# Last two expert tiles kept in SBUF and summed by TensorE, and adjacency loop numbers packed into one register load

## The reference

```python
edge_index = jnp.stack([src, dst])
xn = _layernorm(x, axis=-1)
x = x + _L0_gnn_ref(xn, edge_index, ...) + _L0_mix_ref(xn[None], ...)[0]
x = x + _L0_ffn_ref(_layernorm(x, axis=-1)[None], ...)[0]
...
x = x + _L3_ffn_ref(_layernorm(x, axis=-1)[None], ...)[0]
```

```python
top_w, top_idx = jax.lax.top_k(gate_weights, TOP_K)      # TOP_K = 2 of 8
combine = combine.at[jnp.arange(T)[:, None], top_idx].add(softmax(top_w))
for e in range(E):
    out = out + combine[:, e:e + 1] * (gelu(xf @ we1[e] + be1[e]) @ we2[e] + be2[e])
```

## Time and profile before

| | us |
|---|---|
| median of 3 runs | 3020.09 |
| profiled execution | 3023.55 |
| its span | 3021.8 |
| PE matmuls busy | 2625.2 |
| DVE busy | 1713.8 |
| ACT busy | 1170.1 |
| POOL busy | 1214.3 |
| adjacency, first to last one-hot | 12.7 to 158.5 |
| end of routed layer 1 (last tile scaled) | 2156.1 |
| end of routed layer 2 | 2632.5 |
| end of routed layer 3 | 2982.1 |

### The profile page before, as it was taken

How to read it: one execution, slowest core, us unless ns; L and a number is a source line. 1 busy time by engine, 2 the same in 40 slices (tenths; PEclk the granted TensorE clock), 3 DMA queues, 4 the chain that set the end, 5 groups by cost and what they waited for, 6 DMA issues and landing times. The chain is left out here.

```text
span 3021.8 us, 46495 instructions
## 1 busy us (share of the span) xinstructions
PE 2625.2 (87%) x16977; PEld 1700.5 (56%) x16977; DVE 1713.8 (57%) x3387; ACT 1170.1 (39%) x2632; POOL 1214.3 (40%) x1469
## 2 busy tenths in 40 slices
PE   8899889999978989989898977999699959769684
PEld 5555558556556855545554645777346646445462
DVE  7776778724687863766535353222336376554743
ACT  6454457423546633322412242444232325432141
POOL 0121677877277788855304212111004226510042
PEclk9999999999999999989998987999799979979897
DMA  2001345443044544424101008999701049720297
GB/s 52 14 22 61 112 147 153 137 122 101 32 136 145 156 129 123 126 91 126 39 8 42 28 16 329 412 414 416 247 1 43 29 148 323 252 63 1 70 379 253
DMA packets 164807, 415.38 MB, mean 137 GB/s; under 512 B 24027, under 2 KB 75771, under 8 KB 141356
## 3 DMA queue, kind: packets, MB, share of 16 engines
q1 hardware_dynamic: 150077, 362.10, 35.6%
q0 software_dynamic: 12960, 42.48, 3.7%
q10 hardware_dynamic: 1555, 7.95, 1.1%
HBM read 325.37 MB, written 87.09 MB: 136 GB/s over the span
## 5 line engine op out<-in xcount | busy, mean ns | idle before, releaser
L2924 POOL TENSOR_SCALAR raw<-raw 128x512 f32<-128x512 f32 x376 | 267.2, 711 | 928.6 <-PE ps L527 297.2
L545 PE MATMUL ps<-units,ARENA 128*125 128x512 f16 x2760 | 617.6, 385 | 16.2 <-POOL units L2928 11.4
L527 PE MATMUL ps<-ARENA,units 128*128 128x500 f16 (+1 forms) x2952 | 540.0, 345 | 22.7 <-ACT tmp L1511 6.0
L545 PEld LDWEIGHTS ps<-units,ARENA 128*125 128x125 f16 x2760 | 375.1, 139 | 243.9 <-DVE X L2578 16.4
L527 PEld LDWEIGHTS ps<-ARENA,units 128*128 128x128 f16 x2952 | 289.7, 99 | 271.1 <-issue 22.0
L1969 DVE TENSOR_TENSOR ARENA<-tmp,ARENA 128x500 f16<-128x500 f32 (+3 forms) x237 | 172.1, 732 | 379.2 <-ACT ARENA L1437 191.8
L2928 POOL TENSOR_TENSOR AT<-raw,AT 128x512 f16<-128x512 f32 x200 | 242.2, 1211 | 17.0
L2928 POOL TENSOR_TENSOR units<-raw,units 128x512 f16<-128x512 f32 x188 | 230.4, 1226 | 16.0
L1436 ACT ACTIVATE tmp<-ps,cols 128x500 f32<-128x500 f32 (+1 forms) x144 | 87.5, 608 | 352.2 <-PE ps L527 343.6
L2977 POOL DMA_INDIRECT picks_d<-ARENA,proj x81 | 82.0, 1013 | 341.3 <-DVE ARENA L2421 341.3
L1033 PE MATMUL ps<-ARENA 128*128 128x128 f16 x3240 | 192.0, 220 | 2.2 <-DVE ARENA L2412 2.0
(11 more groups left out here) (480 smaller groups left out, 4479.7 us busy)
## 6 DMA issues: line engine op xcount, KB each, us to landing
ARENA<-split_d SPq DMA_DIRECT2D x135, 1024.0 KB
raw<-in_moe SPq DMA_DIRECT2D x200, 256.0 KB, 3.0
split_d<-AT SPq DMA_DIRECT2D x200, 256.0 KB, 2.5
raw<-in_units SPq DMA_DIRECT2D x188, 256.0 KB, 2.5
ARENA<-split_d SPq DMA_DIRECT2D x27, 1280.0 KB
rows_d<-ARENA SPq DMA_DIRECT2D x6, 896.0 KB
ARENA<-picks_d SPq DMA_DIRECT2D x6, 896.0 KB
ARENA<-picks_d ACTq DMA_DIRECT2D x6, 896.0 KB
```

The costliest lines, as they stand in the source:

```text
L527: ins = pe.matmul(o[:, 0:nt * R], wt, mv_, start=(i == 0), stop=(i == len(steps) - 1))
L545: ins = pe.matmul(o[0:R, :], th(srcT, h, k, t, 1), w(k, g), start=(i == 0), stop=(i == len(steps) - 1))
L2924: pool.tensor_scalar(r, r, WEIGHT_SCALE, gain, ALU.mult, ALU.mult).then_inc(sem("pool_step"), 1)
```

## The change

The packed numbers: one f32 sum per `dt` (first + 128 x groups + 8192 x before) is made by the three matmuls into one row, cast once, and each engine loads one register per `dt` and takes the three numbers out of it with a mask and two shifts. POOL splits unit 0 only after `tables` is 2. The last two tiles (25, 26) are not scattered. ACT writes their weighted high part in f16, DVE the low part (with the sign of high minus low turned by the order of operands: the sum of both is the value), and DVE makes two maps (125 columns for each token tile, 1 where the slot's token is that column's) once at tile 20. The reload of the picks waits for tiles 23 and 24, goes into other buffers (AT for token tiles 0 to 4, ARENA for 5 to 9, the latter after the ring slots there are free), and comes in chunks of 3, 2 and 5. The first 3 token tiles (5 in layer 3) are still added to X by DVE as they arrive. PE then makes for each token tile the sum of both kept tiles through the maps (4 f16 matmuls of 512 columns), and for the rest of the token tiles also both reloaded picks through the f32 identity (2 f32 matmuls of 512 columns); DVE adds PE's bank to X, one instruction per token tile.

```diff
-PICK_CHUNKS = [(0, 2), (2, 4), (6, 4)]
+PICK_CHUNKS = [(0, 3), (3, 2), (5, 5)]
+KEPT = [TILES - 2, TILES - 1]
+FIRST_HALF = T // 2
+MAPS_AT = 20
+SUMMED_BY_DVE = {1: 3, 2: 3, 3: 5}
+SECOND_HALF_AT = {1: 6144, 2: 5120, 3: 0}
...
+        def span_values(eng, dt):
+            packed = eng.value_load(span_i[:, dt:dt + 1], min_val=128, max_val=(T * GROUPS + 1) * 8192)
+            return (packed & 127).with_bounds(...), ((packed >> 7) & 63).with_bounds(...), (packed >> 13).with_bounds(...)
...
         def load_picks(eng, layer, k):
-            for g in (TILES - 2, TILES - 1):
+            for g in (KEPT[0] - 2, KEPT[0] - 1):
                 eng.wait_ge(sem(f"picks_stored{g % 2}"), 16 * pick_stores(layer, g))
             for c, (t0, nt) in enumerate(PICK_CHUNKS):
+                if t0 == FIRST_HALF:
+                    ...
+                        eng.wait_ge(sem(last[0]), last[1])        # ring slots under the second half
...
-            for i, (v, table) in enumerate(((span_first, ident[0:T, 0:T]), (span_len, ident[0:T, 0:T]), (span_len, tri_tiles))):
-                ins = pe.matmul(o[0:1, i * T:(i + 1) * T], v, table, start=True, stop=True)
+            for i, (v, table) in enumerate(((span_first, ident[0:T, 0:T]), (span_len128, ident[0:T, 0:T]), (span_len, tri_tiles))):
+                ins = pe.matmul(o[0:1, 0:T], v, table, start=(i == 0), stop=(i == 2))
...
+            def token_sums(layer, tiles):
+                if 0 in tiles:
+                    pe.wait_ge(sem("routing_step"), s.more("routing_step", 1))
+                    pe.wait_ge(sem("tile_y"), layer * TILES)
+                for t in tiles:
+                    by_dve = t < SUMMED_BY_DVE[layer]
+                    if not by_dve:
+                        chunk = [c for c, (t0, _) in enumerate(PICK_CHUNKS) if t0 <= t][-1]
+                        pe.wait_ge(sem(f"picks_back{chunk}"), 16 * 2 * len(PARTITION_CUTS) * layer)
+                    pe.wait_ge(*left("dve"))
+                    o = bank("dve", "result" if layer == 3 else "read_dve")
+                    for i in range(2):
+                        for h in range(2):
+                            ins = pe.matmul(o[0:R, :], token_maps[layer][i][:, t * R:(t + 1) * R], kept_y[i][:, h, :], ...)
+                    if not by_dve:
+                        for k in range(2):
+                            ins = pe.matmul(o[0:R, :], ident[0:R, 0:R], back(layer, k, t), start=False, stop=(k == 1))
+                    ins.then_inc(sem("filled_dve"), 1)
...
             routed_hidden(1)
+            token_sums(1, range(0, 7))
...
                     for part in range(2):
                         for c, (t0, nt) in enumerate(CH):
                             pe.matmul(columns[k][c][:, 0:nt * R], xs(part, q)[...], at(q, t0 * R, (t0 + nt) * R), ...)
+                    if k == 0 and q < 3:
+                        token_sums(1, [7 + q])
...
             routed_normed()
+            token_sums(2, range(0, 7))
             for k in range(KC):
                 transposed_group(M, "normed", 0, k)
+            token_sums(2, range(7, T))
...
             routed_hidden(3)
+            token_sums(3, range(T))
...
+            def kept_hi(layer, i):
+                act.wait_ge(sem("filled_dve"), kept_banks[layer, KEPT[i]])
+                act.wait_ge(sem(f"picks_stored{KEPT[i] % 2}"), 16 * pick_stores(layer, KEPT[i] - 2))
+                act.activation(kept_y[i][:, 0, :], o[:, :], ACT.Identity, scale=kept_w[:, i:i + 1]).then_inc(sem("tile_hi"), ...)
...
             routed_hidden(1, ACT.Gelu)
+            kept_hi(1, 0)
             load_picks(act, 1, 1)
+            kept_hi(1, 1)
...
-            then(dve.tensor_copy(spans, o[0:1, 0:3 * T]))
-            dve.tensor_copy(span_i[0], spans[:, 0:T])
-            dve.tensor_copy(span_i[1], spans[:, T:2 * T])
-            dve.tensor_copy(span_i[2], spans[:, 2 * T:3 * T]).then_inc(sem("spans"), s.one("spans"))
+            dve.tensor_copy(span_i, o[0:1, 0:T]).then_inc(sem("spans"), s.one("spans"))
...
             def tile_out(layer, g):
...
+                if g in KEPT:
+                    i = g - KEPT[0]
+                    dve.wait_ge(sem("tile_hi"), s.more("tile_hi"))
+                    stt(kept_y[i][:, 1, :], o[:, :], kept_w[:, i:i + 1], kept_y[i][:, 0, :], ALU.mult, ALU.subtract).then_inc(sem("tile_y"), ...)
+                    return
...
+            def early_picks(layer, tiles):
+                for t in tiles:
+                    dve.wait_ge(sem(f"picks_back{chunk}"), 16 * 2 * len(PARTITION_CUTS) * layer)
+                    for k in range(2):
+                        tt(nat(X, t), nat(X, t), back(layer, k, t), ALU.add).then_inc(sem("dve_step"), ...)
+                        dve.wait_ge(*s.latest())
...
                     if g >= 1:
                         tile_out(layer, g - 1)
+                    if g == MAPS_AT:
+                        token_columns(layer)
+                    if g == TILES - 1 and layer == 1:
+                        early_picks(layer, range(SUMMED_BY_DVE[layer]))
+                if layer == 3:
+                    early_picks(layer, range(SUMMED_BY_DVE[layer]))
...
-                        tt(nat(X, t), nat(X, t), nat(back[0], t), ALU.add).then_inc(sem("dve_step"), s.one("dve_step"))
-                        dve.wait_ge(*s.latest())
-                        tt(nat(X, t), nat(X, t), nat(back[1], t), ALU.add).then_inc(sem(name), s.one(name))
+                    dve.wait_ge(sem("filled_dve"), s.more("filled_dve"))
+                    tt(nat(X, t), nat(X, t), s.bank("dve")[0:R, :], ALU.add).then_inc(sem(name), s.one(name))
...
                     if g >= lag:
-                        scatter(g - lag)
+                        if g - lag not in KEPT:
+                            scatter(g - lag)
...
+                if u == 0:
+                    pool.wait_ge(sem("tables"), 2)
```

More of the change, by code:

```diff
@@ L352, in build, with back @@
         mean_sq = ARENA[:, 14408:14409]
-        back = [YT[:, :], ARENA[:, 2 * T * D:3 * T * D]]
+        kept_w = proj[:, 0, 436:438]
+        kept_y = [tile_y[g % 2].bitcast(F16).rearrange("p (h n) -> p h n", h=2) for g in KEPT]
+        token_iota = K[:, 2048:2048 + N // 2].bitcast(F16)
+        token_maps = {layer: [(tmp.rearrange("p i n -> p (i n)") if layer == 2 else K[:, 2673:2673 + N])[:, i * N // 2:(i + 1) * N // 2].bitcast(F16) for i in range(2)]
+                      for layer in (1, 2, 3)}
+        def back(layer, k, t, n=1, p0=0, p1=R):
+            if t < FIRST_HALF:
+                a = XSEL_END + (k * FIRST_HALF + t) * D
+                return AT[p0:p1, a:a + n * D]
+            a = SECOND_HALF_AT[layer] + (k * FIRST_HALF + t - FIRST_HALF) * D
+            return ARENA[p0:p1, a:a + n * D]
+        kept_banks = {}
         unit_release = []
@@ L362, in pick_stores @@
         def pick_stores(layer, g):
-            return (layer - 1) * (TILES - TILES // 2 if g % 2 == 0 else TILES // 2) + g // 2 + 1
+            return (layer - 1) * sum(i % 2 == g % 2 for i in range(TILES - len(KEPT))) + g // 2 + 1
         marks = {}
@@ L398, in load_picks @@
         def load_picks(eng, layer, k):
-            for g in (TILES - 2, TILES - 1):
+            for g in (KEPT[0] - 2, KEPT[0] - 1):
                 eng.wait_ge(sem(f"picks_stored{g % 2}"), 16 * pick_stores(layer, g))
             for c, (t0, nt) in enumerate(PICK_CHUNKS):
+                if t0 == FIRST_HALF:
+                    width = L2_COLS if layer == 2 else 2048
+                    for slot in range(SECOND_HALF_AT[layer] // width, (SECOND_HALF_AT[layer] + 2 * FIRST_HALF * D - 1) // width + 1):
+                        last = [use[4] for use in ring_uses if use[0] == layer and use[1] == slot][-1]
+                        eng.wait_ge(sem(last[0]), last[1])
                 for p0, p1 in PARTITION_CUTS:
-                    eng.dma_start(back[k][p0:p1, t0 * D:(t0 + nt) * D].rearrange("p (t d) -> p t d", t=nt),
+                    eng.dma_start(back(layer, k, t0, nt, p0, p1).rearrange("p (t d) -> p t d", t=nt),
                                   picks_d[k * PICK:k * PICK + N, :].rearrange("(p t) d -> p t d", t=T)[p0:p1, t0:t0 + nt, :])\
@@ L1695, in tile_hi @@
                 act.activation(tile_T[g % 2][:, 0, :, :].rearrange("p k n -> p (k n)"), o[:, :], ACT.Identity).then_inc(sem("tile_hi"), s.one("tile_hi"))
+            def kept_hi(layer, i):
+                act.wait_ge(sem("filled_dve"), kept_banks[layer, KEPT[i]])
+                o = PS[RING["dve"][(kept_banks[layer, KEPT[i]] - 1) % len(RING["dve"])]]
+                act.wait_ge(sem(f"picks_stored{KEPT[i] % 2}"), 16 * pick_stores(layer, KEPT[i] - 2))
+                act.activation(kept_y[i][:, 0, :], o[:, :], ACT.Identity, scale=kept_w[:, i:i + 1]).then_inc(sem("tile_hi"), s.one("tile_hi"))
             def routed_hidden(layer, func):
@@ L1751, in routed_normed @@
                         gelu_squares(h2_rows[(g - 1) % 2], ss2[(g - 1) % 2])
+                    if g == TILES:
```

(4 more changed lines are left out.)

56 lines of the change are left out of this document (33 added, 23 removed).

## The result

| | before | after |
|---|---|---|
| median of 20 runs each, us | 3018.23 | 3006.18 |
| lowest and highest | 3010.80, 3030.53 | 3000.04, 3017.07 |
| ratio, 95% interval | | 0.9965 (0.9953 to 0.9976) |
| span of the profiled execution | 3021.8 | 3004.4 |
| mean granted clock | 0.936 | 0.946 |

What follows compares the result with a forecast made beforehand. PE's matmuls fill 87% of the span, so time is gained only where PE stands still or is paced by others. -6.3 - 5.9 + 6.8 - 4 - 1 = -10.4 from 3020.09: 3009.7 us, range 3000 to 3026.

Steps and rivals of the forecast that it cites:

- POOL out of the adjacency: Adjacency: the tile beside POOL's split of unit 0 falls from 18.67 to 12.33 us; -6.3 us (bounds -7 and -3).
- one load for three: Adjacency: fewer register loads save 0.55 us in each of 9 tiles and 0.9 at the start; -5.9 us.
- layer 1: End of routed layer 1: earlier reload and PE's sums end the block near 2201.5 instead of 2205.3; -4 us.
- layer 2: End of routed layer 2: last chunk about 2653 instead of 2661, third projected tile about as before; -1 us.
- layer 3: End of layer 3: reload issued 4.3 us earlier, but five PE sums follow the last chunk; net +6.8 us.
- Rival (a): Adjacency: masks and shifts eat the loads' gain, at 0.84 us of register work per tile; 3015.6 us, chance 0.17.
- DVE's own saving adds nothing: Adjacency, change of tile: PE's path is the longer one, so DVE's fewer loads give no time.
- by the reload's price the first chunk is there at about 2160: Layer 1: first chunk, three tiles from both halves, at about 2160 after ACT's issue at about 2151.2.
- The price of a reload: Reload of the picks: 2.7 + 4.27 us per MB, from arrivals 7.1, 16.35 and 24.6 us after issue.
- rival (b): Reload gains little, ACT's half held behind tile 25; last chunk some 4 us later per layer; 3021.7 us, chance 0.12.
- Sums 5 and 6 wait for that chunk: Layer 2: PE's sums 5 and 6 wait for the last chunk, at about 2653, and stand ahead of the transposes.
- Rival (c): Layers 2 and 3: clock stays at 1.2 GHz in sums 5 to 9 after chunk waits; +23, 3033 us, chance 0.10.

Runs made afterwards that it cites:

- the kernel with the kept sums first: The changed kernel with DVE adding the kept tiles' sums before the picks in all layers, and all ten tiles' picks in layer 3; ratio 0.9919.
- POOL's wait alone: The kernel before with only POOL's split of unit 0 put behind the adjacency tables; ratio 0.9989 (0.9974 to 1.0003).
- PE's three loads: The changed kernel with PE reading the packed number three times per tile and DVE once; ratio 1.0017 (1.0003 to 1.0030).

## Why the prediction was right, and where not

| step | forecast | measured |
|---|---|---|
| POOL out of the adjacency | -6.3 | -3.1 alone, -7.2 on top of the packed numbers (trace) |
| one load for three | -5.9 | -10.4 (trace), -6.6 (time) |
| layer 1 | -4 | -1.5 |
| layer 2 | -1 | +2.9 |
| layer 3 | +6.8 | +2.7 |
| sum | -10.4 | -13.5 (traces), -10.6 (time, 7 to 14) |

The layers' numbers are differences of means: the pieces of the three kernels without kept tiles (89.3, 55.5 and 39.3) against those of the kernels with them and DVE's order unchanged in that layer (87.7, 58.4 and 42.0; five or six each).

**POOL.** The mechanism was right: the tile gave exactly 18.67 - 12.33. Its size alone was off because I took the other tiles' times for fixed, while the clock isn't. The Trainium skill ("SBUF — State Buffer", Who interferes with whom) says that a fast DVE mode and GpSimd exclude each other on a shared port; the traces agree, down to a POOL TENSOR_TENSOR of 1.27 us beside DVE and 1.15 alone.

**The loads.** Two terms were mis-sized. A load costs 0.6 us, so two give 1.2 per tile on PE where I had 0.84, two thirds of the gap; mask and shifts take back 0.2, near the 0.3 that I had charged, and 0.9 reach the tile's time (12.33 to 11.43) instead of 0.55. Rival (a), which needed 0.84 us of register work, is dead. And "DVE's own saving adds nothing" was wrong for the two long tiles, 3.5 us.

**Layer 3.** The reload left 4.3 us earlier, as worked out (2962.20 is 0.46 ahead of the last expert product, before it was 3.87 behind), the last chunk took 23.15 us instead of 24.6, the five sums and the addition took 15.3 for 16.5 forecast. And the end came 3.8 us behind the last addition instead of 5.8, a term that I had at nothing. The store of tiles 4 to 7 can begin 5.2 us ahead of the last addition, before it was 2.7; in the kernel with the kept sums first it is 2.7 again and the tail 5.9, which speaks for that as the cause. Each term was right to 2 us, and all errors had one sign.

**Layer 1.** The step that failed is "by the reload's price the first chunk is there at about 2160", 9 us behind ACT's issue: it took 13.5. All behind it, DVE's early additions ahead of tile 26 and PE's start, is 3.8 us later for that, and the block ends 2.7 later than I said (both counted from the end of tile 26's product). The price of a reload was read from halves issued at the same moment and didn't hold for halves 4 us apart: that is nearest to rival (b), chance 0.12, though not as it was put: it was the early chunks that came late, and its clause that one half alone does not fill the engines doesn't hold (between the two issues, from 2129 to 2131, the DMA share is 0.99).

**Layer 2.** "Sums 5 and 6 wait for that chunk" failed: they waited for nothing (2636.23). The wait was at sum 3, for chunk 1 and, 1.7 us longer by the two traces, for a bank held behind DVE's early additions. I hadn't counted PE's banks against DVE's order. Behind it PE ran at the low clock until the sum was over (0.50 in the window 2629 to 2633), as counted.

**Rival (c)** did not come: sums 6 to 9 of layer 3 ran at 1.00. The Trainium skill's rule that activity releases the throttle ("TensorE: Matmul & The Clock Gate", What's actually happening) agrees with that.

So the total was right by cancellation: by the traces the adjacency gave 5.4 us more than I said, and the layers cost 2.3 more; the times leave room for either half of it to be smaller.

## What to carry to other kernels

Where two engines hand tiles to each other, price a pause twice: by its length and by what the clock loses behind it; behind pauses of 1.2 to 1.8 us some tiles took 1.6 to 1.8 us more, behind pauses of 0.14 to 0.36 none did. A transfer split over two queues had its price only when both halves left together; where one engine must finish something first, put its issue ahead of it. When work moves from a waiting engine to the one behind the last transfer, count what remains behind that transfer: here five sums of 2.6 us took the place of additions of 1.33 a tile, and giving them back was worth more than the earlier start.

## What the runs showed of the hardware

The granted clock falls within an otherwise busy stretch: windows of 4 us show 0.57 to 0.75 behind PE's pauses at the change of tile, at one place in the kernel before (a second one is beside POOL), three with POOL's wait alone, four with PE's three loads, and at none in the kernel after. Which of the pauses it follows, the runs don't tell. A register load costs PE and DVE 0.6 us each, a mask and two shifts on what it read 0.2 together. Two halves of a reload, 2.56 MB up to the second chunk, take 13.4 to 14.8 us when issued together (four places) and, counted from the first, 20.2 to 21.9 when 2.0 to 2.2 us apart (four places; 18.1 and 18.5 with the last chunk cut in two). Why so small an offset costs 3 to 8 us, the runs leave open. The windows behind the issue, of the kernel before (together) and after (apart):

```profile
2163.00:2168.00 5.00, 0.00 (x0) 0.00 (x0) 1.37 (x2) 1.28 (x1) 0.00 (x0) 0.50 1.05 262
2131.00:2136.00 5.00, 5.00 (x24) 2.21 (x24) 0.75 (x1) 0.67 (x1) 0.00 (x0) 1.00 1.05 262
```

Over 15 to 20 us behind the issue the DMA share was 0.98 to 1.07 in both, so the engines were as busy in the one as in the other. That points to the order in which the bytes came, which no run looked at.
